# Expert mixtures: the gates' weights in two halves side by side, the halves added behind, and the bias on GpSimd

## The reference, cut to what matters

```
logits = x @ W_router.T                 # 8 gates per token
probs = softmax(logits); top 2 kept and divided by their sum -> combine[n, 8]
h  = einsum('nd,erd->ner', x, A)        # 8 experts x 16 numbers = 128 per token
hw = h * combine[:, :, None]
out = x @ W_base.T + b_base + einsum('ner,eor->no', hw, B) * 2
```

## Time and profile before

| | us |
|---|---|
| median of 3 runs | 3356.8 |
| lowest, highest | 3349.62, 3358.44 |
| the profiled execution's own time | 3353.88 |
| its span | 3352.0 |
| mixture of kind 1, first gates' product to the end of the stage | about 904 to 997 |
| mixture of kind 2, the same | about 3188 to 3282 |

### The profile page before, as it was taken

One profiled execution on the slowest core, in us unless ns is written; L12 is line 12 of the kernel. 1 busy time (PEld: TensorE's weight loads), 2 busy tenths in 40 slices (PEclk: granted clock), 3 DMA queues, 4 the chain that ended last, 5 costly groups with the idle time before them and its releaser, 6 DMA issues. The chain is left out here.

```text
span 3352.0 us, 70367 instructions
## 1 busy us (share of the span) xinstructions
PE 3239.0 (97%) x22206; PEld 2989.2 (89%) x22206; DVE 2484.1 (74%) x6389; ACT 1838.9 (55%) x4523; POOL 1589.4 (47%) x2658
## 2 busy tenths in 40 slices
PE   6799999999899999999899999999999999999999
PEld 5688899988778888888899999999999999788877
DVE  6445644445477778878899999989999999688874
ACT  4323322233227877878666666666666666655522
POOL 0231100000007878888677777767777776043102
PEclk9899999999999999999999999999999999999999
DMA  5413432334555555556767776756777677888753
GB/s 208 138 55 75 126 83 81 85 107 132 182 171 172 179 173 173 180 179 202 245 235 241 240 245 234 240 198 229 240 241 240 234 245 239 298 306 302 260 186 104
DMA packets 406731, 645.41 MB, mean 193 GB/s; under 512 B 43289, under 2 KB 275545, under 8 KB 389466
## 3 DMA queue, kind: packets, MB, share of 16 engines
q1 hardware_dynamic: 386650, 502.49, 44.8%
q0 software_dynamic: 19712, 138.42, 12.8%
HBM read 440.74 MB, written 200.02 MB: 191 GB/s over the span
## 5 line engine op out<-in xcount | busy, mean ns | idle before, releaser
L2654 PE MATMUL l2a_x<-l2a_pt,l2a_V 128*128 128x128 f32 x4096 | 542.3, 275 | 2.6 <-DVE l2a_pn L2588 1.7
L2654 PEld LDWEIGHTS l2a_x<-l2a_pt,l2a_V 128*128 128x128 f32 x4096 | 498.6, 192 | 3.7 <-issue 3.6
L2566 DVE CUSTOM_DVE_ANT_0 l2a_sm<-l2a_s,l2a_B 128x544 f32<-128x544 f32 x512 | 367.4, 718 | 71.0 <-PE l2a_s L199 64.2
L2520 ACT ACTIVATE l2a_p<-l2a_sm,l2a_st 128x544 f32<-128x544 f32 x512 | 380.5, 743 | 43.1 <-DVE l2a_st L2566 42.9
L2346 POOL CAST keys<-cache 128x256 fp32r x750 | 303.1, 451 | 187.7 <-issue 159.0
L2505 ACT ACTIVATE l2a_pt<-l2a_t 128x512 f32<-128x512 f32 x512 | 304.2, 594 | 89.7 <-PE l2a_t L2637 87.4
L2578 DVE TENSOR_SCALAR l2a_p<-l2a_p,l2a_st 128x512 f32<-128x512 f32 x512 | 308.2, 602 | 18.3
L2637 PE MATMUL l2a_t<-ident,l2a_p 128*128 128x128 f32 x2048 | 307.9, 273 | 5.2 <-ACT l2a_quads L2513 5.2
L2346 POOL CAST l2a_K<-cache 128x256 fp32r x768 | 305.0, 445 | 16.2 <-issue 16.2
L2513 ACT ACTIVATE l2a_quads<-l2a_x 128x128 f32<-128x128 f32 x512 | 142.1, 278 | 278.7 <-PE l2a_x L2655 278.7
L2069 POOL MEMSET l2q_eps<- 128x5 f32 x1 | 0.1, 104 | 620.4 <-DMA s_x<-moe_xr 620.4
(11 more groups left out here) (1028 smaller groups left out, 8979.7 us busy)
## 6 DMA issues: line engine op xcount, KB each, us to landing
s_qT<-l2q_qo SPq DMA_DIRECT2D x128, 512.0 KB, 2.9
part<-s_ao SPq DMA_DIRECT2D x28, 2048.0 KB, 10.3
head<-s_qT SPq DMA_DIRECT2D x64, 512.0 KB, 6.1
l2a_Q<-s_qT SPq DMA_DIRECT2D x64, 512.0 KB
s_ao<-l2a_combos SPq DMA_DIRECT2D x64, 512.0 KB
s_kn<-l2q_ko SPq DMA_DIRECT2D x128, 128.0 KB, 2.9
head<-s_kn SPq DMA_DIRECT2D x32, 512.0 KB, 5.8
s_ao<-l2a_quads SPq DMA_DIRECT2D x64, 256.0 KB, 2.2
```

The source lines that it names most:

```text
L2520: act.activation(prr[sc % 6][:, :].rearrange("p (k g j) -> p g k j", k=4, j=8), smr[sc % 2][:, :].rearrange("p (g k j) -> p g k j", k=4, j ...
L2566: dve.tensor_tensor_reduce(out=smr[sc % 2][:, :], in0=ps_s[sc % 2][:, 224:768], in1=Br[g % 2][:, :], scale=-SCALE, scalar=3e38, op0=ALU.ad ...
L2654: pe.matmul(px[:, P:256], V[:, k * D + hg * P:k * D + hg * P + P], pt[:, k, :], start=k == 0, stop=False)
```

## The change

The gates' weights are laid out per block of 128 inputs as high part and low part side by side, so that one product with the input's high part gives both halves, 276 wide (kind 1) or 272 wide (kind 2). A second, narrow product adds low x high onto the first half. Four pairs of products take the place of twelve products. The two halves lie in one PSUM tile and are added behind: ScalarE copies the second half to `hw` (`halves`), VectorE adds the first half onto it (semaphore `summed`). The gates, and h for the multiplication with them, are now read from `hw` in SBUF and no longer from `pl` in PSUM, and `hw` is 138 or 136 wide. TensorE reuses `pl` after `summed`, no longer after `weighed`. The bias addition moves from VectorE to a new GpSimd stream.

```diff
@@ Ahead
-        self.gates = tuple(room[:, z * n:z * n + n].rearrange("p (k n) -> p k n", k=4) for z in range(2))
+        sides = room[:, 0:2 * n].rearrange("p (k z n) -> p k z n", k=4, z=2)
+        self.gates = tuple(sides[:, :, z, :] for z in range(2))
+        self.both = room[:, 0:2 * n].rearrange("p (k n) -> p k n", k=4)
@@ moe
+        @block.gpsimd
+        def _(pool):
+            pool.wait_ge(bias_in, 16)
+            for tt in range(NT):
+                pool.wait_ge(*xr.landed(tt, 1))
+                pool.tensor_tensor(xr[tt][:, :], xr[tt][:, :], bias[:, :], ALU.add).then_inc(biased, 1)
@@ scalar
+            def halves(tt):
+                if tt < NT:
+                    act.wait_ge(gate_mm, tt + 1)
+                    if tt >= 8:
+                        act.wait_ge(turned, tt - 7)
...
+                    act.activation(hw[tt % 8][:, :], pl[tt % 4][:, n:2 * n], ACT.Copy).then_inc(half, 1)
...
             for tt in range(NT):
                 parts(tt + 4)
                 gates(tt + 2)
+                halves(tt + 3)
                 lora(tt + 1)
                 beside.on_scalar(act, tt, pl)
@@ vector, gates
-                    dve.wait_ge(gate_mm, tt + 1)
+                    dve.wait_ge(half, tt + 1)
+                    dve.tensor_tensor(h[:, :], h[:, :], ps[:, 0:n], ALU.add).then_inc(summed, 1)
+                    dve.wait_ge(summed, tt + 1)
                     if tt >= 4:
                         dve.wait_ge(weighed, tt - 3)
-                    (sigmoid_gates if kind == 1 else top2_gates)(tt, s, ps[:, 0:8])
+                    (sigmoid_gates if kind == 1 else top2_gates)(tt, s, h[:, 0:8])
...
-                dve.tensor_tensor(h[:, :]..., ps[:, G:G + P]..., s[:, 32:40]..., ALU.mult).then_inc(weighed, 1)
+                dve.tensor_tensor(h[:, G:n]..., h[:, G:n]..., s[:, 32:40]..., ALU.mult).then_inc(weighed, 1)
-            def with_bias(tt):
...
-                with_bias(tt + 1)
@@ tensor, gates
-                        pe.wait_ge(weighed, tt - 3)
-                    mm3(pe, pl[tt % 4][:, 0:G + P], [... for k in range(4)]).then_inc(gate_mm, 1)
+                        pe.wait_ge(summed, tt - 3)
+                    high, low = dT[tt % 8]
+                    for k in range(4):
+                        pe.matmul(pl[tt % 4][:, 0:2 * n], high[:, k, :], both[:, k, :], start=k == 0, stop=False)
+                        i = pe.matmul(pl[tt % 4][:, 0:n], low[:, k, :], gc[0][:, k, :], start=False, stop=k == 3)
+                    i.then_inc(gate_mm, 1)
```

More of the change, by code:

```diff
@@ L1496, in on_scalar, with on_tensor @@
             act.activation(self.xT[t][0], banks[t][:, :].rearrange("p (k n) -> p k n", k=4), ACT.Copy).then_inc(self.hi, 1)
-    def on_tensor(self, pe, tt, banks, weighed):
+    def on_tensor(self, pe, tt, banks, summed):
         if 11 <= tt < 13:
@@ L1502, in on_tensor @@
             pe.wait_ge(*self.nat.landed(t))
-            pe.wait_ge(weighed, 13 + t)
+            pe.wait_ge(summed, 13 + t)
             for k in range(4):
@@ L1652, in on_tensor @@
                 pe.wait_ge(self.b_lo, 1)
-            pe.wait_ge(weighed, 13 + k)
+            pe.wait_ge(summed, 13 + k)
             mm3(pe, banks[k][:, :], [(sl(self.a3, S_, m, slice(k * P, (k + 1) * P)), sl(self.b3, S_, m, S_))
@@ L1680, in moe @@
     bt = pair("bt", [P, 1, D])
-    gc = S["ahead"].gates
+    gc, both = S["ahead"].gates, S["ahead"].both
+    n = G + P
     dT = S["ahead"].dT + [pair(f"dT{i}", [P, 4, P]) for i in range(3, 8)]
@@ L1688, in moe @@
     ix = [st.sb(f"ix{i}", [P, 8], U32) for i in range(2)]
-    hw = [st.sb(f"hw{i}", [P, P]) for i in range(8)]
+    hw = [st.sb(f"hw{i}", [P, n]) for i in range(8)]
     hT = [st.pair(f"hT{i}", [P, P]) for i in range(4)]
@@ L1705, in moe @@
     turned, h_hi, h_lo, out_mm, biased, added = (st.sem(n) for n in ("turned", "h_hi", "h_lo", "out_mm", "biased", "added"))
-    step = st.sem("step")
+    step, half, summed = (st.sem(z) for z in ("step", "half", "summed"))
     before_d = S["d_stores"]
@@ L1757, in parts @@
                     act.activation(dT[tt % 8][0][:, :, :], dr[tt - 3][:, :, :], ACT.Copy).then_inc(d_hi, 1)
+            def halves(tt):
[3 more added lines that the diff above has]
+                        act.wait_ge(turned, tt - 7)
+                        act.wait_ge(exped, tt - 7)
+                        if kind == 1:
+                            act.wait_ge(tanhed, tt - 7)
+                    act.activation(hw[tt % 8][:, :], pl[tt % 4][:, n:2 * n], ACT.Copy).then_inc(half, 1)
             def gates(tt):
                 if tt < NT:
-                    s, lg = sm[tt % 4], pl[tt % 4]
+                    s, lg = sm[tt % 4], hw[tt % 8]
                     act.wait_ge(topped, tt + 1)
@@ L1779, in _ @@
                 w.high(act, k)
+            halves(0)
             gates(0)
             w.high(act, 4)
+            halves(1)
             gates(1)
+            halves(2)
             parts(3)
@@ L1859, in lora @@
                     low_part(dve, sl(hT[tt % 4], S_, S_), pt[tt % 2][:, 0:P]).then_inc(h_lo, 1)
-            def with_bias(tt):
-                if tt < NT:
-                    dve.wait_ge(*xr.landed(tt, 1))
-                    dve.tensor_tensor(xr[tt][:, :], xr[tt][:, :], bias[:, :], ALU.add).then_inc(biased, 1)
             if kind == 1:
@@ L1875, in _ @@
             lora(0)
-            dve.wait_ge(bias_in, 16)
-            with_bias(0)
             for tt in range(NT):
@@ L1903, in lora @@
                         pe.wait_ge(h_lo, tt - 1)
-                    pe.transpose(pt[tt % 2][:, 0:P], hw[tt % 8][:, :], ident[:, :]).then_inc(turned, 1)
+                    pe.transpose(pt[tt % 2][:, 0:P], hw[tt % 8][:, G:n], ident[:, :]).then_inc(turned, 1)
             def whole(tt):
@@ L1926, in _ @@
                 lora(tt + 1)
-                beside.on_tensor(pe, tt, pl, weighed)
+                beside.on_tensor(pe, tt, pl, summed)
             if kind == 2:
```

5 lines of the change are left out of this document (1 added, 4 removed).

## The result

| | before | changed |
|---|---|---|
| median, us | 3356.83 (10 runs) | 3360.14 (10 runs) |
| lowest, highest | 3348.27, 3359.41 | 3355.8, 3367.75 |
| profiled execution, its span | 3353.88, 3352.0 | 3359.0, 3357.2 |

The ratio of the changed kernel to the one before is 1.0018, 95% interval 1.001 to 1.0027. That is about 6 us slower, under the 0.3% within which the prediction counted "same", and 3360 lies inside the range of 3347 to 3366.

The account below looks back on a forecast made before the run. Two loops were taken to share the time: TensorE's work and a chain through ScalarE and VectorE. Mixtures +0.65 and +0.6, last tiles -0.6, starts +0.6 and +1.0, end -0.3 gave +2.0 us; named 3357, range 3347 to 3366.

Parts of the forecast that it names:

- the part without collisions: Whole change if GpSimd and VectorE never get in each other's way: -6.2 us.
- The gates' product: On TensorE, 1.29 us per tile falls to 0.97, saving 0.32 (bounds 0.30 and 0.43).
- p: TensorE's own work per tile: 4.89 us before, forecast 4.57 in the first mixture and 4.55 in the second.
- Rival 3: The wide gates' product costs what one 512 wide does, 1.38 us per tile: +7.7, 3361.6; chance 0.08.
- The halves in L: ScalarE's copy 0.10 and VectorE's addition 0.34 enter L, the bias's 0.61 leaves: 5.30 to 5.13, second mixture 4.76.
- L: Loop from a tile's transpose through ScalarE and VectorE to the start of `whole` two tiles on: 5.30 us before.
- Rival 1: No collision between GpSimd and VectorE in the mixtures: -6.2 us, 3347.7; chance 0.17.
- rival 4: VectorE's loop falls under TensorE's and all waits go: -11.1 us, 3342.8; chance 0.03.
- Collisions in the loops: GpSimd's bias addition delays VectorE by 0.6 us per tile (bounds 0 and 1.26), all of it in L.
- half of itself: In the mixtures' tiles, a gain or loss in either of the two loops counts half per tile.
- rival 2: GpSimd's addition stops VectorE's whole gate chain for 1.26 us in each tile: +12.2, 3366.1; chance 0.14.
- The starts: At each mixture's start, 0.3 us for the halves and 0.5 for four GpSimd additions in a row, both twice.

Follow-up runs that it names:

- e3: Changed kernel with the bias addition of both mixtures left out, so GpSimd is idle there: 3346.4 us, ratio 0.9975 to the kernel before.
- e1: Changed kernel with the bias addition back on VectorE, gates' product still in halves: 3354.5 us, ratio 0.9998.
- e9: Changed kernel with a third PSUM bank for the tiles' results, GpSimd's additions behind the input's low part in the first mixture: 3342.1 us, ratio 0.9964.
- e5: Changed kernel with GpSimd's additions held only until VectorE has made the first input low part: 3363.0 us, ratio 1.0023.
- e12: Kernel before with only the bias moved to GpSimd, each addition placed behind the next tile's gates' multiplication: 3348.7 us, ratio 0.9983.
- e10: Kernel before with only a third PSUM bank for the tiles' results, bias on VectorE: 3351.2 us, ratio 0.9982.
- e7: Changed kernel with a third PSUM bank and GpSimd's additions placed behind the next tile's gates' multiplication: 3341.3 us, ratio 0.9954.
- e8: Changed kernel with a third PSUM bank and the bias on VectorE: 3345.7 us, ratio 0.9971.

## Why the prediction was right, and which of its steps were not

The time fell into the range, and the part without collisions was right: -6.2 us forecast, -5.6 in e3's trace by the two mixtures (184.9 us against 190.5), -8 by ratio. The price of the collisions was short: 8.2 us forecast, 12.7 between e3's trace and the changed kernel's, 14 by ratio. Of the 12.7 the loops have 8.2 (7.2 forecast) and the starts 4.6 (1.0 forecast). That the answer still came out as "same" is partly luck, since the missing 4 to 6 us are less than the 10 us that the prediction couldn't tell from no change.

- **The gates' product.** Forecast 0.97 us, measured 0.91: a pair of products 276 and 138 wide costs about 0.24 (0.91 from 940.63 to 941.54 is four pairs, the first of them 0.19). p became 4.50, not 4.57. Rival 3 is out.
- **The halves in L.** Right: 5.13 forecast for L without collisions, 5.14 in e3; with the bias back, 5.74 against 5.72 in e1. In the second mixture e3's tiles without extra work took about 4.57 in place of 4.655.
- **Rival 1 and rival 4.** Not what happened. Without any addition of the bias the changed kernel gains 8 us (e3, ratio 0.9975), which is between the two rivals' prices, 6.2 and 11.1.
- **Collisions in the loops.** The size was right, its make-up was not. Forecast: 0.6 in each tile, half of which counts, 0.3 per tile. Measured in the first mixture: 61.71 - 57.83 = 3.9 us over twelve tiles between the changed kernel and e3, 0.32 per tile. But they are five holds of 0.77 in the mean (3.85 in all), and each counted in full. The rule "half of itself" holds for a delay that comes in every tile; with short and long tiles in turn, a single delay of a long tile shifts all that follows by its whole length. That the equal sums come of this is argued from the two loops, and no run places a single hold. In the second mixture 7.3 us of holds cost 4.3; the forecast said 3.3.
- **Which operations are held.** This step failed. The prediction counted operations with two large SBUF inputs, the input's low part and the multiplication with the gates, and left the small operations to rival 2 because no row showed them. 13 of the 21 holds are on operations of one to eight elements, held by up to 1.12 of GpSimd's 1.28. That is rival 2's mechanism. Its price, +12.2, is not reached, because the additions start with the landings and fall on a small operation only in some tiles, and because sums, reciprocals and all that read PSUM pass.
- **The starts.** The term that was mis-sized. Forecast: 0.3 for the halves and 0.5 for the burst, twice, 1.6 us in all. Measured: +2.6 and +4.0. The halves cost 0.7 at each start, not 0.3 (second transpose behind the first by 7.71 and 8.90 in e3, 7.00 and 8.20 before), and 0.1 and 0.5 lie ahead of the first transpose. The rest, 1.8 and 2.8 us, is what the changed kernel has over e3. In the first mixture 1.5 of the 1.8 stand in the slower products. e9 has the same 4.61 there with its first addition on GpSimd only at 920.64, 0.72 behind their start, so a held VectorE isn't needed for them. In the second the holds at 3199.04 and 3200.39 are 1.95, and 0.7 stand in slower products (5.10 from 3202.20 to the next group, 4.40 in e3).
- **The ends.** Forecast 0.6 and 0.3 faster, measured 0.85 and 0.4.
- **"The two stages should change by under 2 us each"** was wrong: +3.2 and +3.9 (first gates' product to the next stage: 95.5 to 98.7 and 95.0 to 98.9). The chip's answer stayed within "same" because 7 us are still 0.2%.

On the page "SBUF — State Buffer", section "SBUF: two separate sides", of the Trainium skill: the part of its rule that the prediction kept apart, operations in a two-port mode, would fit the eight-element holds here (1.25 for 0.29 beside GpSimd in e5). Its part on operations with two SBUF inputs sets no size; "large" was the prediction's own word. That part fits the one-element SCALAR_TENSOR_TENSOR, which has two SBUF inputs and was held in e5, while one-element TENSOR_SCALARs, with one input, passed. Operations with an input in PSUM went free in every case here (0.69 at 3208.19, inside an addition).

What stays open: what sets TensorE's clock at the second tile's base products in the first mixture. With 1.83 us of idle time ahead of them they took 3.06 (before), 3.06 (e12) and 5.49 (e10); with 2.94 to 3.19, 3.06 (e1, e3), 4.60 (e7), 4.61 (e9) and 4.59 (changed). The idle time ahead alone doesn't decide it, and it moves a kernel by up to 2.4 us. Of the eight kernels with additions on GpSimd all but e12 have 4.4 to 4.6 there, and of the six without all but e10 have 3.06. With one traced execution each that can be chance, and no run tests it. Also open is VectorE's wait for the load of `iota` at 3195.62, 1.66 us: e3, without any GpSimd stream here, has one of 1.68 at the same place.

## What to carry to other kernels

Before moving elementwise work to GpSimd, list what VectorE does while it would run: operations that read PSUM go on, and so do sums and reciprocals inside SBUF; copies, subtractions and small operations with scalars inside SBUF may stand until GpSimd's instruction ends. If there is a stretch that reads PSUM, tie GpSimd's start to it with a semaphore; that one wait was worth 14 us here (ratio 1.0018 to 0.9976), and 13 on the kernel before (1.0023 to 0.9983), while a wait that only shifts the burst (e5) made it no better. And when a product gets cheaper, look for the second loop that its result passes through: here the halves took 0.38 from one loop and put about 0.4 into the other. With a third bank, which takes that loop away, twelve tiles were 2 to 3 us shorter with them (e8 against e10), and the whole time about 4, which the runs don't separate from nothing.

## What the hardware did that I had not expected

- A VectorE operation on 128x8 elements with SBUF operands took up to 1.35 us for 0.23 beside GpSimd's addition (914.87), and a copy of 128x8 was held as well, 0.64 for 0.15, at 3204.35.
- Holding goes the other way too: GpSimd's addition that began 0.01 behind VectorE's low part took 1.81 for 1.28. Row of GpSimd, changed kernel:

```profile
953.08 1.81 POOL L1758 TENSOR_TENSOR moe_xr<-moe_xr,moe_bias 128x512 f32<-128x512 f32 x1 [4.64 <-DMA moe_xr<-s_x]
```

- The same twelve products, with the same wait of 1.83 us ahead of them, took 3.06 in one kernel and 5.49 in another.
